# Causal attention inside a fused transformer kernel: half of the heads masked after the exponential by GpSimd instead of by TensorE, and a stage's GpSimd work laid out in smaller pieces

## The reference, cut to what matters

```python
def _L3_attn_ref(hidden_states, w_attn, b_attn, w_proj, b_proj):
    H, D = 16, 8
    NEG = -1000000000.0
    ...
    w = jnp.einsum('bhnd,bhmd->bhnm', q, k) * jax.lax.rsqrt(float(D))
    mask = jnp.tril(jnp.ones((S, S), dtype=jnp.float32))
    w = jnp.where(mask > 0, w, NEG)
    w = jax.nn.softmax(w, axis=-1)
    attn = jnp.einsum('bhnm,bhmd->bhnd', w, v)
    attn = attn.transpose(0, 2, 1, 3).reshape(B, S, E)
    return attn @ w_proj.T + b_proj
```

## Time and profile before

| | us |
|---|---|
| median of 3 runs | 2948.27 |
| lowest and highest of them | 2932.73, 2956.56 |
| the profiled execution, whole | 2950.33 |
| its span on the engines | 2948.4 |
| attention 3, first load issued to last logits copied | 2218 to 2573 |

### The profile page before, as it was taken

The page is one execution under the profiler, slowest core; times in us unless marked ns, Lnnn a source line. Parts: engine busy times, 40 slices in busy tenths (PEclk is TensorE's granted clock), DMA queues, the critical chain, the costliest instruction groups (busy, mean ns, idle before and its releaser), DMA issues. The chain is left out here.

```text
span 2948.4 us, 52675 instructions
## 1 busy us (share of the span) xinstructions
PE 2350.3 (80%) x17978; PEld 1648.9 (56%) x17978; DVE 1449.3 (49%) x4042; ACT 1478.3 (50%) x3688; POOL 1331.5 (45%) x2068
## 2 busy tenths in 40 slices
PE   6999999994567999980599589996996999736850
PEld 4666666663554666650599345553553777524840
DVE  3555555553117999963233365672003666320743
ACT  4666666662336999970122156674222666512421
POOL 2444444443227888645533565531003454153255
PEclk9999999997776999995799698898997999967975
DMA  3000000002113222103111232220002322020212
GB/s 135 1 1 1 1 1 1 1 1 75 59 60 96 74 72 72 53 1 123 46 51 48 77 118 83 77 67 7 0 0 78 104 89 89 13 66 31 87 59 60
DMA packets 100389, 153.43 MB, mean 52 GB/s; under 512 B 16851, under 2 KB 69989, under 8 KB 93093
## 3 DMA queue, kind: packets, MB, share of 16 engines
q1 hardware_dynamic: 88356, 128.32, 13.7%
q0 software_dynamic: 11776, 21.81, 2.4%
HBM read 99.85 MB, written 48.24 MB: 50 GB/s over the span
## 5 line engine op out<-in xcount | busy, mean ns | idle before, releaser
L980 DVE TENSOR_REDUCE A_nmax<-A_S 128x2 f32<-128x512 f32 (+1 forms) x512 | 309.0, 620 | 220.8 <-PE A_S L766 110.9
L181 POOL TENSOR_SCALAR A_prob<-A_prob,A_rinv 128x256 f32<-128x256 f32 x512 | 235.4, 478 | 371.4 <-DVE A_rinv L433 371.4
L911 ACT ACTIVATE A_PT<-A_E 128x512 f32<-128x512 f32 (+1 forms) x512 | 275.2, 546 | 161.0 <-PE A_E L783 82.2
L428 DVE TENSOR_REDUCE A_nmax<-A_S 128x2 f32<-128x512 f32 x256 | 164.8, 685 | 161.0 <-PE A_S L271 161.0
L371 ACT ACTIVATE A_prob<-A_S,A_nmax 128x256 f32<-128x256 f32 x512 | 234.8, 477 | 4.9 <-DVE A_nmax L428 4.9
L1797 POOL COPY L_wr<-L_w 128x1024 f32 (+1 forms) x144 | 104.1, 724 | 240.8 <-PE L_k L1871 124.2
L1790 POOL DMA_INDIRECT sent<-x_state,row x160 | 154.6, 967 | 118.5 <-DVEq L2046 70.6
L1562 DVE TENSOR_SCALAR_CACHE_REDUCE A_D<-A_S 128x256 f32<-128x256 f32 x512 | 193.5, 417 | 15.8 <-PE A_S L1345 11.0
L1568 DVE COPY A_PT<-A_T 128x512 f32<-128x512 f32 x256 | 175.1, 686 | 20.1 <-PE A_T L1358 19.8
L1358 PE MATMUL A_T<-ident_sb,A_D 128*128 128x128 f32 x1024 | 161.1, 281 | 27.9 <-ACT A_D L1487 14.9
L1964 ACT ACTIVATE L_silus<-L_k 128x512 f32<-128x512 f32 x72 | 43.0, 597 | 261.3 <-PE L_k L1867 261.3
(11 more groups left out here) (382 smaller groups left out, 6030.8 us busy)
## 6 DMA issues: line engine op xcount, KB each, us to landing
A_QS<-stack_q SPq DMA_DIRECT2D x144, 192.0 KB
A_KS<-stack_k SPq DMA_DIRECT2D x144, 192.0 KB
L_xe<-sent SPq DMA_DIRECT2D x46, 256.0 KB
results<-L_ye SPq DMA_DIRECT2D x46, 256.0 KB
stack_q<-A_parts SPq DMA_DIRECT2D x48, 192.0 KB
stack_k<-A_parts SPq DMA_DIRECT2D x48, 192.0 KB
L_w<-f_w SPq DMA_DIRECT2D x24, 256.0 KB, 10.6
sent<-A_zeros SPq DMA_DIRECT2D x9, 512.0 KB
```

What stands on the lines that cost most here:

```text
L181: nc.gpsimd.tensor_scalar(prob[:, n % NP, j, t, :], prob[:, n % NP, j, t, :], rinv[:, n % NP, j, t:t + 1], 1.0, ALU.mult, ALU.mult).then_i ...
L428: nc.vector.tensor_reduce(nmax[:, n % NP, j, :], psS[n % 2][j][:], AX.X, ALU.max, negate=True).then_inc(maxed, 1)
L911: nc.scalar.activation(PT[:, n % RING, :], psE[n % 2][:, 0:BLOCKS, :].rearrange("p a b -> p (a b)"), ACT.Exp, scale=scale).then_inc(expd, 1)
L980: nc.vector.tensor_reduce(nmax[:, b % 2, :, h], view, AX.X, ALU.max, negate=True).then_inc(maxed, 1)
```

## The change

In attention 3 every head with an even n (`by_select`) loses the two mask products of the second score. Its exponentials are taken unmasked, and GpSimd overwrites those of later keys with zero in both diagonal blocks, by one `affine_select` of 128 x 2 x 128 fp32 elements in place in `PT` (`mask_later`), in slot n + 31. It waits for the head's exponentials. `weigh` now waits for the selects of its four heads as well as for their exponentials. The first score keeps its masks, for the row maxima need them.

In both attentions the four instructions of `split_qk` are issued in four slots, one a slot, where they were issued in one.

In attention 3 `LAG_PV` grows from 33 to 36, which moves `weigh`, `take_o`, `turn_o`, `normalise`, `turn_on`, `project_out`, the norm and `add_out_bias` back by three slots; `turn_new` and the logits move by 12 (3 + 9). `turn_new` waits for earlier logits to be copied out of psX.

```diff
-    LAG_PV = LAG_E + 3
+    LAG_PV = LAG_E + (6 if causal else 3)
...
-    F_AT, LG_AT = Y_AT + 11, Y_AT + 13
+    F_AT = Y_AT + (20 if causal else 11)
+    LG_AT = F_AT + 2
...
-    FIRST, LAST = GET_AT, SLOTS + Y_AT
+    FIRST, LAST = GET_AT, SLOTS - H + LG_AT + 3
...
+        def by_select(n):
+            return n % 2 == 0
+
+        def selects(n):
+            return (n + 1) // 2
...
-                def split_qk(b):
+                def split_qk(b, step):
                     i = b % 2
-                    pool.wait_ge(qk_ready, 2 * (b + 1))
-                    after(pool, stored[i], 32 * (b // 2))
-                    nc.gpsimd.tensor_copy(parts[:, i, 0, :], qk[:, i, :]).then_inc(split, 1)
-                    pool.wait_ge(split, 4 * b + 1)
...
+                    if step == 0:
+                        pool.wait_ge(qk_ready, 2 * (b + 1))
+                        after(pool, stored[i], 32 * (b // 2))
+                        nc.gpsimd.tensor_copy(parts[:, i, 0, :], qk[:, i, :]).then_inc(split, 1)
+                        return
+                    pool.wait_ge(split, 4 * b + step)
...
+                def mask_later(n):
+                    pool.wait_ge(expd, n + 1)
+                    p = PT[:, n % RING, :].rearrange("p (t c) -> p t c", c=P)[:, 0:BLOCKS:2, :]
+                    nc.gpsimd.affine_select(p, p, [[0, 2], [1, P]], ALU.is_ge, 0.0, base=0, channel_multiplier=-1).then_inc(masked, 1)
...
+                    if causal and (n := head(s, LAG_E + 1)) is not None and by_select(n):
+                        mask_later(n)
...
-                    if (b := at(s, QK_AT + 3)) is not None:
-                        split_qk(b)
+                    for step in range(4):
+                        if (b := at(s, QK_AT + 3 + step)) is not None:
+                            split_qk(b, step)
...
-                        nc.tensor.matmul(S[:, 0:2, :].rearrange("p a b -> p (a b)"), k[:, 0:P], q, start=True, stop=False)
-                        nc.tensor.matmul(S[:, 0, :], consts["maskb"][:], consts["identb"][:], start=False, stop=True)
-                        nc.tensor.matmul(S[:, 2, :], k[:, P:], q[:, P:], start=True, stop=False)
-                        i = nc.tensor.matmul(S[:, 2, :], consts["maskb"][:], consts["identb"][:], start=False, stop=True)
+                        by_pe = not by_select(n)
+                        nc.tensor.matmul(S[:, 0:2, :].rearrange("p a b -> p (a b)"), k[:, 0:P], q, start=True, stop=not by_pe)
+                        if by_pe:
+                            nc.tensor.matmul(S[:, 0, :], consts["maskb"][:], consts["identb"][:], start=False, stop=True)
+                        i = nc.tensor.matmul(S[:, 2, :], k[:, P:], q[:, P:], start=True, stop=not by_pe)
+                        if by_pe:
+                            i = nc.tensor.matmul(S[:, 2, :], consts["maskb"][:], consts["identb"][:], start=False, stop=True)
...
                         pe.wait_ge(expd, H * b + 4 * g + 4)
+                        if causal:
+                            pe.wait_ge(masked, selects(H * b + 4 * g + 4))
...
                     pe.wait_ge(v_ready, before(V_AT + 1, H * b + F_AT))
+                    if onward["gate"] is not None:
+                        after(pe, lg_out, before(LG_AT, H * b + F_AT))
```

More of the change, by code:

```diff
@@ L506, in attention_small @@
     RUN = ROWS + PARTS
-    NBUF, RING, NV = 5, 12, 6
+    NBUF, RING, NV = 5, 12 if causal else 12, 6
     LAG_E = 30
-    LAG_PV = LAG_E + 3
+    LAG_PV = LAG_E + (6 if causal else 3)
     LAG_O = LAG_PV + 2
@@ L563, in attention_small @@
         nm_split, nm_psum, nm_ready, nm_in = sem("nm_split"), sem("nm_psum"), sem("nm_ready"), sem("nm_in")
-        turned, expd, weighed, o_ready = sem("turned"), sem("expd"), sem("weighed"), sem("o_ready")
+        turned, expd, masked, weighed, o_ready = sem("turned"), sem("expd"), sem("masked"), sem("weighed"), sem("o_ready")
         ot_psum, inverted, normed, on_psum, on_ready = sem("ot_psum"), sem("inverted"), sem("normed"), sem("on_psum"), sem("on_ready")
@@ L634, in _ @@
                 pool.wait_ge(loaded, LOADED)
-                def split_qk(b):
+                def split_qk(b, step):
                     i = b % 2
-                    pool.wait_ge(qk_ready, 2 * (b + 1))
-                    after(pool, stored[i], 32 * (b // 2))
-                    nc.gpsimd.tensor_copy(parts[:, i, 0, :], qk[:, i, :]).then_inc(split, 1)
-                    pool.wait_ge(split, 4 * b + 1)
[L642 to L646, removed]
+                    if step == 0:
[4 more added lines that the diff above has]
+                    pool.wait_ge(split, 4 * b + step)
+                    if step == 1:
+                        nc.gpsimd.tensor_tensor(rest[:], qk[:, i, :], parts[:, i, 0, :], ALU.subtract).then_inc(split, 1)
+                    elif step == 2:
+                        nc.gpsimd.tensor_copy(parts[:, i, 1, :], rest[:]).then_inc(split, 1)
+                    else:
+                        nc.gpsimd.tensor_tensor(parts[:, i, 2, :], rest[:], parts[:, i, 1, :], ALU.subtract).then_inc(split, 1)
                 def split_max(b):
```

## The result

The changed kernel took 2924.86 us (median of 20 runs, 2911.67 to 2935.15) against 2946.98 us (20 runs, 2932.73 to 2962.44) before. The ratio is 0.9928, interval 0.9915 to 0.9941: 21 us less, where 13 were forecast. The profiled execution took 2925.58 us, where that of before took 2950.33; its span is 2923.9 us.

What follows compares the result with a forecast made beforehand. TensorE was taken to bound attention 3's full stretch. Removed products 15.0 us, less 0.9 at the end and 0.5 for waits, gave 13.6, rounded to 13: median from 2948.3 to 2935 us, range 2921 to 2968.

Steps and rivals of the forecast that it cites:

- The products: TensorE's second scores in attention 3: 128 heads lose a pair at 0.117 us, 15.0 us, less 0.9 at the end.
- The select: GpSimd's new instruction in attention 3: 0.6 us, 0.67 with its gap, bounded by 0.41 and 1.37.
- GpSimd's room: Attention 3's full stretch: 16.1 us a sequence with eight selects fits TensorE's 17.4, with 1.3 us to spare.
- Splitting q and k a piece a slot matters here: GpSimd's burst in attention 3: four pieces in one slot would put 3.8 us ahead of each of two selects.
- The point of 0.77 us without a gap: Select length at which GpSimd ceases to fit in TensorE's sequence of attention 3; 0.84 us with the gap.
- The maxima's DMA: Attention 3's full stretch: issued 0.4 us earlier, about 1.1 us of cover remain; costed at nothing, up to 1 a sequence.
- The end is even: End of attention 3: 1.5 us come back from the unblocked last turn, against about 0.9 and 0.5 us added.
- Attention 2: Its split ends 2.4 us later, but its DMAs have some 25 slots, so costed at 0.
- GpSimd as the bound: Rival in attention 3's full stretch: select of 0.85 to 1.1 us, result between 2940 and 2958; chance 0.24.
- the select as slow as the bound: Rival: `weigh` waits for selects all through attention 3, 2981 at 1.37 us; with the clock down, above 2960; chance 0.12.
- the branching select: Rival on GpSimd: select branches per element, 2.6 to 2.7 us each, kernel at 3150; chance 0.03.
- TensorE gains more than the products: Rival on TensorE: 81 ns a product or a shorter stall behind VectorE gives 2928; chance 0.03.

Runs made afterwards that it cites:

- the moves alone: Changed kernel with no head selected, all mask products kept, later offsets and spread split kept: 0.9991 of the kernel before, attention 3 at 351.4 us.
- the select twice: Changed kernel with every select done a second time, waiting for the first: 0.9925 of the kernel before, 17.37 us a sequence.
- third set: Another chip, kernel before 2879.36 us: changed kernel 0.9939, with attention 2's split together 0.9942; every head selected, split spread 0.9916, together 0.9910.
- first comparison: Changed kernel timed against the kernel before, 20 runs each: 2924.86 against 2946.98 us, ratio 0.9928.
- attention 3 only: Changed kernel, but attention 2 keeps its split of q and k in one slot: 0.9946 of the kernel before, later 0.9942 on another chip.
- all heads: Changed kernel with all 256 heads of attention 3 selected, no mask product in the second score: 0.9911 of the kernel before, later 0.9916 on another chip.
- first two sets: Variants of the changed kernel, each set on one chip and timed against the kernel before in it; ratios from 0.9911 to 0.9991.

## Why the prediction was right, step by step

The run is 21 us faster, 13 were forecast, and the range (2921 to 2968) holds its 2924.86. The band held likeliest, 2928 to 2941, does not, and the excess is not of the forecast's making: some 2.5 us come from the moves, which it put at nothing, and 5 stand outside attention 3. The mechanism is what the runs showed (products leave a full TensorE, and GpSimd has room for the selects); the terms measured as follows.

- **The products.** Forecast 15.0 less 0.9 at the end less 0.5 for waits, less 0.6 by rounding. From the moves alone to the whole change attention 3 loses 13.4 us, and a pair costs 0.119 us against the 0.117 used; 128 pairs would be 15.2. The last 30 second scores take 22.19 us from the first start to the last where the moves alone have 23.05, so 0.9 of their 1.8 us are lost, as forecast. More is lost where the forecast named no place: the last three periods fall by 0.87, 0.63 and 0.52 us (16.44, 16.43, 14.90 to 15.57, 15.80, 14.38) instead of three times 0.95, and the first four by 2.3 where their 28 pairs would bring 3.3. Against this 0.6 us come behind the last score. The 0.5 for waits and the rounding covered it. "TensorE: Matmul & The Clock Gate" of the Trainium skill, section "Back-to-back issue gap", has 81 ns for a product of 128 columns in a stream with weight loads, and by another formula of that section, meant for isolated products, about 56 ns at the full clock. The rows and the experiments agree with the second, 0.06, in a stream of weight loads and products.
- **The select.** Taken at 0.6 us between bounds of 0.41 and 1.37; it is 0.409, the price of the copy of the same shape (0.408), below the 0.5 to 0.75 that the forecast wanted to see, and 0.35 to 0.37 from start to start. Of the two rows of its shape the cheaper one was right, not L181 (0.478), which the forecast called nearest; the addition for the comparison and the gap of 0.07 were not there either. The error had no price, since GpSimd was not the bound. The rule of "GPSIMD Engine Reference" of the Trainium skill, section "Performance versus the Vector engine", on data-dependent branching does not apply to this instruction: it would have given an estimated 2.6 us.
- **GpSimd's room.** Fit was right, with more to spare: the forecast had 1.3 us a sequence left, the profile shows 53.6 us of waits for ScalarE over 202, 4.6 a sequence of 17.35. "Splitting q and k a piece a slot matters here" was wrong at 0.41 us: with the pieces in one slot nothing changes. The point of 0.77 us without a gap was too near: at 0.82 a head (the select twice) TensorE's sequence is longer by 0.02 us. It went by gaps that aren't there. From the wait that is left an estimate of the point is 0.36 + 4.6 / 8 = 0.94 us a head from start to start; no run reached it.
- **The maxima's DMA.** Costed at nothing, and no second score of the full stretch waits for it. The time from issue to reading fell from 7.45 to 7.03 us; the forecast had it fall by 0.4.
- **The moves.** "The end is even" is the step in attention 3 that was mis-sized: the forecast counted only what stands behind the last score. The moves bring 2.5 us: 3.5 between the second scores and 0.2 ahead of the first, less 1.2 behind the last. That they could shorten the sequences themselves was left out of the sum.
- **Attention 2.** Costed at nothing. On the third set's chip that is what it was, to 0.06%, and the whole change brings 0.61% there, 17.6 us. In the first comparison 15.9 of the 21 us are in attention 3, and that is below the interval for the whole (17 to 25 us). So a part of the remaining 5 would be real there and stand outside attention 3, by a narrow margin and by one profile of each kernel; whether it belongs to the change, no run shows. Whether the spread pieces lower the count of long sequences on a chip that has them stays open: the profiles lean to it (mean 390.6 us in eight profiles with the pieces spread, 404.5 in two that have them together), the timed runs say 0.1% with an interval of 0.18% either way.

The rivals: GpSimd as the bound, the select as slow as the bound and the branching select all hang on a select of over 0.77 us, and fell with 0.409. "TensorE gains more than the products" (2928) is nearest to the outcome, though for another reason than the ones it gave: not a dearer product, but the moves and what stands outside attention 3.

## What to carry to other kernels

When the bounding engine is full at its full clock, a removed instruction is worth its spacing in the stream, here to 2%, and this goes on until another engine answers late. Here twelve selects of sixteen paid in full in the full stretch, and with sixteen four pairs brought 0.10 us instead of 0.48; it was VectorE's maxima that came late, not GpSimd, which had taken the work. An operation that the trace doesn't show is priced by the row with the same tile, inputs and outputs before anything is added for what it computes. A stage that shows another time in each profile, as attention 2 here, is judged by timed runs with the one edit in it, on more than one chip, and not by two profiles.

## What was not expected

- The new instruction's duration is not its price in a row: 0.409 us long, 0.35 to 0.37 from start to start, two in 0.77.
- Attention 2 of three kernels (changed, attention 3 only, all heads) took 384 to 402 us in the first comparison and the first two sets, and 373 to 377 on the third set's chip, where no full sequence was long: TensorE was busy 37.50 of 40 us at clock 1.00 there, and 36.48 at 0.90 in the first comparison. Nor does the busy share tell the clock: in the profile of before, the 40 us from 1880 on had 37.98 us of work at 0.75, and in the changed kernel 37.21 at 1.00. The first is 264 products and the second 342: at the lower clock fewer products fill the same time.

```profile
1880.00:1920.00 40.00, 37.98 (x264) 21.94 (x264) 23.21 (x53) 24.58 (x57) 20.87 (x40) 0.75 0.22 69
```

```profile
1880.00:1920.00 40.00, 37.21 (x342) 22.43 (x338) 29.00 (x70) 30.09 (x71) 22.36 (x44) 1.00 0.32 93
```

- Attention 3, with TensorE full, took nearly the same time in the first comparison and on the third set's chip: 338.0 and 338.6 us for the changed kernel, 17.35 us a sequence.
